# Two engines take up the first tile's copies and shares ahead of splitting the first expert's first chunk

## The chip, the cores and the metric
The kernel runs on one core of a Trainium2 chip. The metric is the device time of one execution in microseconds (us), as the median of several; the profile is of one further execution. The five engines run their own instruction streams and meet only at semaphores: TensorE (PE, with its weight loads shown as PEld), VectorE (DVE), ScalarE (ACT), GpSimd (POOL) and SyncE (SP, which here only issues transfers). Each engine takes its instructions in the order in which the program gives them, so an instruction that waits holds up all that stands behind it on its engine.

## The reference
1024 rows (32 batches of 32) of width 1024 go through three blocks. Each adds its result to the rows.

```python
def _L0_attn_ref(minibatch, eta):                 # the second block, "mixing"
    logits = jnp.einsum('bcl,bdl->bcd', minibatch, minibatch)
    logits_new = jnp.max(logits, axis=-1, keepdims=True) - logits
    probs = jax.nn.softmax(logits_new, axis=-1)
    read = jnp.einsum('bcd,bdl->bcl', probs, minibatch)
    return eta * read + minibatch

x = x + _L0_xattn_ref(_layernorm(x), ctx_4096, ctx_4096, Wq, Wk, Wv, Wo)
x = x + _L0_attn_ref(_layernorm(x), eta)
x = x + _L0_ffn_ref(_layernorm(x), gate_w, expert_w)   # 8 experts, the best 2 of each row
```

The first block is cross attention over a context of 257 rows a batch, the last a mixture of eight experts, each a 1024 x 1024 product.

## The kernel before
All products that matter are made from float32 split in two parts of less precision, a high one (a rounded copy, made by ACT) and a low one (what is left, a subtraction on DVE), and three passes: high by high, high by low, low by high. `attend` is the attention up to its output projection. `finish` does the rest for eight tiles of 128 rows (NT = 8), and this case lies in its first loop, the mixing stage. Every engine runs that loop over t and in each step serves up to three tiles at once, in an order written out by hand:

- PE (from `for t in range(1, NT)`): the output projection of tile t, `product(t, unit)`, in eight units of six matmuls of 512 columns (L1554). Between the units stand, for earlier tiles, `mix(t - 2)` ahead of unit 2 (L1588, L1594), `turn_y(t - 1)` ahead of unit 4 (eight transposes, L1566), `rank(t - 2)` ahead of unit 5 and `products_of_rows(t - 1)` ahead of unit 6 (64 small matmuls, L1578). `turn_y` writes the turned rows to PSUM, `products_of_rows` needs them in SBUF, as yT.
- ACT (L1277 on): `ot_high(t + 1)` splits the next tile's attention output (L1221), `first_high(0, t - 1)` makes the high part of one 128 x 1024 chunk of the first expert's weights (L1256), `copy_y(t - 1)` copies the turned rows to yT (L1228), `exp_gap`, `normalize_n`, then `shares(t - 1)` takes the exponentials of the products (L1244).
- DVE (L1455 on): the second half of x2 = x + projection (`add_x(t - 1, 1)`, L1338), its moments (L1344, L1348), `normalize_y` (L1353), the mixing sum and the routing of tile t - 2, `ot_low(t + 1)` (L1329), `first_low(0, t - 1)`, which is the low part of the expert's chunk (L1438), `add_x(t, 0)`, `rank_tile(t - 2)` and `turn_shares(t - 1)`, which takes the least product of each row (low, L1418), waits for ACT's exponentials, turns them (probT, L1424) and makes the scales up to L1432.
- SP: after the attention four small loads of the gate's weights into yT (L1035), one of eta (L1036), a clearing store, then the eight chunks of the first expert (L1025), and from there one row tile of x a step (`load_x(t + 1)`, L1022).
- POOL: the powers for the norms, the sum of x2 and y, and the scattering of routing entries.

`first_high(0, 0)` waits until chunk 0 of the expert has been loaded. The loads of the expert can't start before the attention is over, since they use its memory. At t = 1 there is no tile t - 2 yet, so `mix`, `rank` and their partners on the other engines fall away.

After the mixing stage the rows are gathered by expert and multiplied, tile by tile (L1624 for the first three tiles, L1708 for the others, with transposes at L1615).

Of the kernel before, what the change touches and what calls it, by code (L numbers as in the profile page):

```python
# [29 lines left out]
NT = B * SQ // P  # L30
# [858 lines left out]
def finish(nc, sh, x, eta, gate, expert_w, out, n_dram, slot_dram):  # L889
# [6 lines left out]
    with ExitStack() as ctx:  # L896
# [91 lines left out]
        def on(t, lag):  # L988

            return 0 <= t - lag < NT  # L990
# [226 lines left out]
        def _(act):  # L1217
            def ot_high(t):
                if t >= 2:
                    act.wait_ge(xo_done, 2 * t - 2)  # L1220
                act.activation(ot[0][:, t % 2, :, :], oT[:, t, :, :], ACT.Copy).then_inc(ot_h_ready, 1)  # L1221

            def copy_y(t):
                if t >= 1:
                    act.wait_ge(g_done, t)
                for h in range(2):
                    act.wait_ge(t_done, 2 * t + h + 1)
                    act.activation(yT[:, 4 * h:4 * h + 4, :, 0:SQ], t_ps[h][:, :].rearrange("p (k b q) -> p k b q", k=4, q=SQ),  # L1228
                                   ACT.Copy).then_inc(t_copied, 1)

            def exp_gap(t):
                act.wait_ge(gap_ready, t + 1)
                act.wait_ge(rstd3_ready, t + 1)
                act.activation(egap[:, :], gap[:, :], ACT.Exp, scale=rstd3[:, 0:1]).then_inc(egap_ready, 1)

            def normalize_n(t):
                if t >= 2:
                    act.wait_ge(x3_stored[t % 2], 32 * (t // 2))
                act.wait_ge(shift3_ready, t + 1)
                act.activation(n[:, t % 2, :], x3[:, t % 2, :], ACT.Identity, bias=shift3[:, 0:1], scale=rstd3[:, 0:1]).then_inc(n_ready, 1)  # L1240

            def shares(t):
                act.wait_ge(low_ready, t + 1)
                act.activation(prob[:, :], g_ps[:, 0:SQ], ACT.Exp, bias=low[:, 0:1], scale=-1.0,  # L1244
                               accum_out=psum_row[:, :]).then_inc(prob_ready, 1)

            def first_high(e, *chunks):
                for c in chunks:
                    if e == 0:
                        if c == 0:  # L1250
                            act.wait_ge(xo_done, 2)
                        act.wait_ge(ot_l_ready, c + 1)
                    else:
                        act.wait_ge(xo_done, 2 * NT)
                    act.wait_ge(chunk_loaded[c], 48 + 16 * e)
                    act.activation(w[0][:, e * SLOT + c * D:e * SLOT + (c + 1) * D], first_raw[e][:, c, :], ACT.Copy).then_inc(w_h_ready, 1)  # L1256

            def rows_high(i, par):
                if known(i) and i < 2:
                    act.wait_ge(xo_done, 2 * NT - 2 + 2 * i)  # L1260
                else:
                    act.wait_ge(y_done, 2 * i - 2)
                for h in range(2):
                    act.wait_ge(gT_done, 2 * i + h + 1)
                    act.activation(gT[0][:, par, h * 512:(h + 1) * 512], t_ps[h][:, :], ACT.Copy).then_inc(gT_h_ready, 1)  # L1265
# [11 lines left out]
            for t in range(NT + 2):  # L1277
                if 1 <= t and t + 1 < NT:
                    ot_high(t + 1)
                if 1 <= t < NT:  # L1280
                    first_high(0, t - 1)
                if t == NT - 1:
                    first_high(0, NT - 1)
                if t == NT:
                    rows_high(0, 0)
                if on(t, 1):
                    copy_y(t - 1)
                if on(t, 2):
                    exp_gap(t - 2)
                    normalize_n(t - 2)  # L1290
                if on(t, 1):
                    shares(t - 1)
                if t == NT:
                    first_high(1, 0, 1, 2, 3)
# [31 lines left out]
        def _(dve):  # L1326
# [4 lines left out]
            def add_x(t, h):  # L1331
                par = t % 2
                cols = slice(h * 512, (h + 1) * 512)
                dve.wait_ge(x_loaded[par], 16 * (t // 2) + 16)
                if t >= 2:
                    dve.wait_ge(u_ready, 2 * t - 2)
                dve.wait_ge(xo_done, 2 * t + h + 1)
                dve.tensor_tensor(x2[:, par, cols], o_ps[h][:, :], x_in[:, par, cols], ALU.add).then_inc(x2_ready, 1)  # L1338

            def moments(t):  # L1340
                par = t % 2
                for h in range(2):
                    dve.wait_ge(x2_ready, 2 * t + h + 1)
                    dve.bn_stats(stats2[:, h, :], x2[:, par, h * 512:(h + 1) * 512]).then_inc(stats2_ready, 1)  # L1344
                dve.wait_ge(stats2_ready, 2 * t + 2)
                if t >= 1:
                    dve.wait_ge(std_ready, t)
                dve.bn_aggr(mean_var2[:, :], stats2[:, :, :].rearrange("p a b -> p (a b)")).then_inc(var2_ready, 1)  # L1348
# [63 lines left out]
            def turn_shares(t):  # L1412
                par = t % 2
                if t == 0:
                    dve.wait_ge(consts, 16)
                    dve.wait_ge(small_loaded, 16 * (BT + 1))
                dve.wait_ge(g_done, t + 1)
                dve.tensor_reduce(low[:, :], g_ps[:, 0:SQ], AXX, ALU.min).then_inc(low_ready, 1)  # L1418
                dve.wait_ge(prob_ready, t + 1)
                if t >= 1:  # L1420
                    dve.wait_ge(mix_done, t)
                for b in range(BT):
                    q = slice(b * SQ, (b + 1) * SQ)
                    o = dve.transpose(probT[q, q], prob[q, :])  # L1424
                o.then_inc(probT_ready, 1)
                dve.tensor_tensor(gated[:, par, :], g_ps[:, SQ:GW], zero8[:, :], ALU.add).then_inc(gated_ready, 1)
                dve.wait_ge(std_ready, t + 1)
                dve.tensor_tensor(scaled_gated[:, par, :], g_ps[:, SQ:GW], std_plus_one[:, par, :].to_broadcast([P, E]),
                                  ALU.mult).then_inc(gated_ready, 1)
                dve.reciprocal(scale[:, par, :], psum_row[:, :]).then_inc(psr_ready, 1)  # L1430
                dve.wait_ge(psr_ready, t + 1)
                dve.tensor_tensor(scale[:, par, :], scale[:, par, :], eta_sb[:, :], ALU.mult).then_inc(scale_ready, 1)  # L1432

            def first_low(e, *chunks):
                for c in chunks:
                    high, rest = (part[:, e * SLOT + c * D:e * SLOT + (c + 1) * D] for part in w)
                    dve.wait_ge(w_h_ready, KC * e + c + 1)
                    dve.tensor_tensor(rest, first_raw[e][:, c, :], high.bitcast(F32), ALU.subtract).then_inc(w_l_ready, 1)  # L1438
# [10 lines left out]
            def rows_low(i, par):  # L1449
                for h in range(2):  # L1450
                    dve.wait_ge(gT_h_ready, 2 * i + h + 1)
                    dve.tensor_tensor(gT[1][:, par, h * 512:(h + 1) * 512], t_ps[h][:, :],  # L1452
                                      gT[0][:, par, h * 512:(h + 1) * 512].bitcast(F32), ALU.subtract).then_inc(gT_l_ready, 1)

            for t in range(NT + 2):  # L1455
                if on(t, 1):
                    add_x(t - 1, 1)
                    moments(t - 1)
                    if t == EARLY + 2:
                        pad_first_tiles()  # L1460
                    if t == NT:
                        rows_low(0, 0)
                    normalize_y(t - 1)
                if on(t, 2):
                    add_mixed(t - 2)
                    route_tile(t - 2)
                if 1 <= t and t + 1 < NT:
                    ot_low(t + 1)
                if 1 <= t < NT:
                    first_low(0, t - 1)  # L1470
                if t < NT:
                    add_x(t, 0)
                if on(t, 2) and t < NT:
                    rank_tile(t - 2)
                if t == NT - 1:
                    first_low(0, NT - 1)
                if on(t, 1):
                    turn_shares(t - 1)
                if t == NT:
                    first_low(1, 0)  # L1480
                if t >= NT:
                    rank_tile(t - 2)
                if t == NT:
                    first_low(1, 1)
# [270 lines left out]
```

## Time and profile before

| | |
|---|---|
| median of 3 runs | 1076.35 us (1076.14 to 1076.91) |
| the profiled execution | 1077.07 us, of which its span (first to last instruction) 1075.4 us |
| busy: PE / PEld | 1046.3 us (97%) / 957.9 us (89%) |
| busy: DVE / ACT / POOL | 630.2 (59%) / 477.4 (44%) / 242.3 us (23%) |
| mean granted TensorE clock | 0.992 of full speed |

A row of a timeline gives the start in us from the span's first instruction, the duration in us, the engine, the line, the operation, what it writes and reads, its count, and in brackets how long its engine sat idle before it and what ended that. The chain of waits is followed back from the last instruction: at each point, what released the work that stood there. Matmuls are pipelined, and their durations overlap; the distance from start to start says more than a duration.

### The profile page before, as it was taken

How to read it: one execution, taken by the hardware profiler on the slowest of the kernel's cores; microseconds unless marked ns; L12 is line 12 of the kernel's file. 1: busy time of each engine (PE TensorE's matmuls, PEld its weight loads, DVE VectorE, ACT ScalarE, POOL GpSimd, SP SyncE). 2: the span in 40 equal slices, each digit the busy share in tenths (PEclk: the TensorE clock that was granted, in tenths of full speed). 3: DMA queues.
4: the chain of work that ended last, by engine and by line, in shares of the span. 5: the costliest groups of instructions: out<-in, count | busy, mean ns of one | idle time of the engine just before them, and what ended most of it. 6: DMA issues, size and time to landing. Idle time of an engine off the chain costs nothing.

```text
span 1075.4 us, 25383 instructions
## 1 busy us (share of the span) xinstructions
PE 1046.3 (97%) x9043; PEld 957.9 (89%) x9044; DVE 630.2 (59%) x1623; ACT 477.4 (44%) x1129; POOL 242.3 (23%) x412
## 2 busy tenths in 40 slices
PE   9999999999999999999999999899997899999996
PEld 9999999999999999999999999677775788888885
DVE  6641366666666666666766668757778244354220
ACT  4321255455555545555555555523235154454331
POOL 2000212121212121121212121135444323322232
PEclk9999999999999999999999999999999899999998
DMA  9424686656565757575756757365537677588332
GB/s 345 140 79 154 182 246 190 173 184 181 176 192 171 199 171 202 156 209 157 207 155 200 226 152 199 85 238 99 91 127 235 198 227 256 132 259 254 87 77 38
DMA packets 78603, 189.46 MB, mean 176 GB/s; under 512 B 16512, under 2 KB 27136, under 8 KB 74400
## 3 DMA queue, kind: packets, MB, share of 16 engines
q1 hardware_dynamic: 64096, 154.15, 46.6%
q0 software_dynamic: 14400, 33.88, 13.0%
q8 instruction: 69, 1.13, 0.5%
q14 instruction: 38, 0.31, 0.1%
HBM read 148.66 MB, written 44.56 MB: 180 GB/s over the span
## 4 chain that ended last, share of the span: by engine, by line
PE 90%; DMA 3%; DVE 3%; issue 2%; POOL 1%; ACT 1%; SPq 0%; POOLq 0%; DVEq 0%; ACTq 0%
PE bank L1708 18%; PE bank L728 17%; PE bank L719 17%; PE bank L680 9%; PE bank L1554 6%; PE bank L767 6%; PE bank L711 5%; PE bank L786 4%; PE bank L856 3%; PE bank L1615 2%; PE bank L1624 1%; DMA xg<-n_scratch,idx 1%; DMA expert_raw<-in_expert_w 1%; PE bank L756 1%; PE bank L1588 1%
## 5 line engine op out<-in xcount | busy, mean ns | idle before, releaser
L487 ACT ACTIVATE prob<-bank,nmax 128x257 f32<-128x257 f32 x256 | 122.1, 477 | 235.7 <-DVE nmax L635 235.7
L635 DVE TENSOR_REDUCE nmax<-bank 128x1 f32<-128x257 f32 x256 | 108.9, 425 | 151.8 <-PE bank L856 151.8
L728 PE MATMUL bank<-wkv_h,cT_h 128*128 128x256 f32 x512 | 154.5, 302 | 0.0
L719 PE MATMUL bank<-cT_h,wkv_h 128*128 128x256 f32 x512 | 154.3, 301 | 0.0
L728 PE MATMUL bank<-wkv_h,cT_l 128*128 128x256 f32 x512 | 144.6, 282 | 0.0
L719 PE MATMUL bank<-cT_h,wkv_l 128*128 128x256 f32 x512 | 144.3, 282 | 0.0
L728 PE MATMUL bank<-wkv_l,cT_h 128*128 128x256 f32 x512 | 144.1, 282 | 0.0
L719 PE MATMUL bank<-cT_l,wkv_h 128*128 128x256 f32 x512 | 144.0, 281 | 0.0
L382 POOL DMA_DIRECT2D qcat<-q_scratch x128 | 70.5, 557 | 271.5 <-PE bank L856 268.4
L1708 PE MATMUL bank<-w_h,rows_h 128*128 x272 | 108.7, 400 | 0.0
L1708 PE MATMUL bank<-w_l,rows_h 128*128 x272 | 107.3, 394 | 0.0
L1708 PE MATMUL bank<-w_h,rows_l 128*128 x272 | 107.3, 394 | 0.0
L767 PE MATMUL bank<-ident,prob 128*128 128x128 f32 x512 | 99.6, 276 | 3.6 <-DVE pT L273 1.9
L1452 DVE TENSOR_TENSOR rows_l<-bank,rows_h 128x512 fp32r<-128x512 f32 x42 | 27.0, 684 | 127.5 <-ACT rows_h L1265 127.4
L728 PEld LDWEIGHTS bank<-wkv_h,cT_h 128*128 128x128 f32 x512 | 97.4, 190 | 0.0
L627 DVE TENSOR_SCALAR prob<-prob,rsums 128x257 f32<-128x257 f32 x256 | 92.0, 359 | 9.1
L719 PEld LDWEIGHTS bank<-cT_l,wkv_h 128*128 128x128 f32 x512 | 97.2, 190 | 0.0
L728 PEld LDWEIGHTS bank<-wkv_l,cT_h 128*128 128x128 f32 x512 | 97.1, 190 | 0.0
L719 PEld LDWEIGHTS bank<-cT_h,wkv_h 128*128 128x128 f32 x512 | 96.9, 189 | 0.0
L719 PEld LDWEIGHTS bank<-cT_h,wkv_l 128*128 128x128 f32 x512 | 96.8, 189 | 0.0
L728 PEld LDWEIGHTS bank<-wkv_h,cT_l 128*128 128x128 f32 x512 | 96.7, 189 | 0.0
L569 DVE TENSOR_TENSOR cT_l<-bank,cT_h 128x512 fp32r<-128x512 f32 x128 | 87.1, 682 | 10.1 <-ACT cT_h L442 10.1
(213 smaller groups left out, 2377.2 us busy)
## 6 DMA issues: line engine op xcount, KB each, us to landing
kcat<-k_scratch SPq DMA_DIRECT2D x128, 258.0 KB, 4.4
cx<-in_context SPq DMA_DIRECT2D x32, 1024.0 KB, 6.8
raw<-in_expert_w SPq DMA_DIRECT2D x48, 512.0 KB, 7.3
qcat<-q_scratch POOLq DMA_DIRECT2D x128, 128.0 KB, 3.1
k_scratch<-kT_h SPq DMA_DIRECT2D x32, 258.0 KB, 2.4
k_scratch<-kT_l SPq DMA_DIRECT2D x32, 258.0 KB, 2.6
x_in<-in_x SPq DMA_DIRECT2D x16, 512.0 KB, 7.6
expert_raw<-in_expert_w SPq DMA_DIRECT2D x16, 512.0 KB, 8.1
```

The lines of the kernel that those rows point to most:

```text
L382: pool.dma_start(qcat[c * DH:(c + 1) * DH, par, :, :].rearrange("d (g j) n -> d g (j n)", g=4).bitcast(F32), q_dram[c // 2, b].rearrange(" ...
L487: act.activation(prob[1 - par][:, s, 0:SK], s_ps[s % 2][:, 0:SK], ACT.Exp, bias=nmax[:, 1 - par, s:s + 1], accum_out=sums[:, 1 - par, s:s ...
L569: dve.tensor_tensor(cT[1][:, b % 2, 2 * m:2 * m + 2, :].rearrange("p a n -> p (a n)"), cT_ps[m % 2][:, :], high, ALU.subtract).then_inc(cT ...
L627: dve.tensor_scalar(prob[a % 2][:, i, 0:SK], prob[a % 2][:, i, 0:SK], rsums[:, i:i + 1], None, ALU.mult).then_inc(prob_ready, 1)
L635: dve.reduce_max(nmax[:, 1 - par, s:s + 1], s_ps[s % 2][:, 0:SK], AXX, negate=True).then_inc(max_done, 1)
L680: o = pe.matmul(q_ps(UNITS * g + u)[:, m % 2 * GT:(m % 2 + 1) * GT], wq_s[w][:, k, m * P:(m + 1) * P], xT[g % 2][t][:, k, :], start=(m % 2 ...
L711: o = pe.transpose(cT_ps[m % 2][:, n * P:(n + 1) * P], cx[:, b % 2, a, k * P:(k + 1) * P], ident[:, :])
L719: o = pe.matmul(k_ps[:, j * 256:(j + 1) * 256], wkv[w][:, k, j * P:(j + 1) * P], cT[t][:, b % 2, k, :], start=(j == 0 and k == 0 and n == ...
L728: o = pe.matmul(v_ps[:, a * KV:(a + 1) * KV], cT[t][:, b % 2, k, a * P:(a + 1) * P], wkv[w][:, k, KV:2 * KV], start=(a == 0 and k == 0 and ...
L767: o = pe.transpose(turn_ps[:, c * P:(c + 1) * P], prob[a % 2][:, i, c * P:(c + 1) * P], ident[:, :])
L1554: o = pe.matmul(o_ps[h][:, :], ot[a][:, t % 2, k, :], wo_s[b][k][:, h * 512:(h + 1) * 512], start=(k == 0 and m == 0), stop=(k == KC - 1 a ...
L1708: o = pe.matmul(y_ps[par][h][:, :], gT[a][:, par, k * P:(k + 1) * P], w[b][:, bass.ds(slot_at + (k * D + h * 512), 512)], start=(k == 0 an ...
```

## The change
On ACT and on DVE, in step t = 1 alone, the split of the first expert's chunk 0 moves behind other work. ACT now does `copy_y(0)` and then `first_high(0, 0)`, ahead of `shares(0)`. DVE now does `first_low(0, 0)` at the end of the step, behind `add_x(1, 0)` and `turn_shares(0)`. From t = 2 on the order is the old one. No instruction is added or removed.

```diff
@@ ScalarE
-                if 1 <= t < NT:
+                if 2 <= t < NT:
                     first_high(0, t - 1)
                 if t == NT - 1:
                     first_high(0, NT - 1)
@@
                 if on(t, 1):
                     copy_y(t - 1)
+                if t == 1:
+                    first_high(0, 0)
                 if on(t, 2):
                     exp_gap(t - 2)
                     normalize_n(t - 2)
@@ VectorE
                 if 1 <= t and t + 1 < NT:
                     ot_low(t + 1)
-                if 1 <= t < NT:
+                if 2 <= t < NT:
                     first_low(0, t - 1)
                 if t < NT:
                     add_x(t, 0)
@@
                 if on(t, 1):
                     turn_shares(t - 1)
+                if t == 1:
+                    first_low(0, 0)
                 if t == NT:
                     first_low(1, 0)
```

## Rows read from the trace of the kernel before

**Rows 1.** The page, chain that ended last: shares of the span by engine.
```profile
PE 90%; DMA 3%; DVE 3%; issue 2%; POOL 1%; ACT 1%; SPq 0%; POOLq 0%; DVEq 0%; ACTq 0%
```

**Rows 2.** Windows: busy us of each engine (instructions), clock, DMA share, GB/s.
```profile
703.95:706.28 2.33, 0.07 (x1) 0.00 (x0) 0.99 (x1) 2.03 (x3) 0.00 (x0) 1.00 1.02 417
706.28:711.46 5.18, 5.18 (x77) 4.18 (x78) 2.30 (x11) 0.38 (x2) 0.00 (x0) 0.67 1.03 418
711.46:726.80 15.34, 15.34 (x132) 11.89 (x131) 12.14 (x38) 4.79 (x8) 6.87 (x10) 1.00 0.36 134
```

**Rows 3.** Timeline of PE, steps t = 1 and t = 2 of mixing.
```profile
700.19 1.03 PE L1566 MATMUL bank<-ident,y 128*128 128x128 f32 x8
...
703.62 0.40 PE L1554 MATMUL bank<-wo_h,rows_l 128*128 128x512 f32 x1
706.28 0.80 PE L1578 MATMUL bank<-yT 128*32 128x40 f32 x64 [2.27 <-ACT yT L1228]
...
711.46 0.40 PE L1554 MATMUL bank<-wo_h,rows_h 128*128 128x512 f32 x1
...
714.25 1.88 PE L1588 MATMUL bank<-y,probT 128*128 128x512 f32 x4
...
718.97 1.03 PE L1566 MATMUL bank<-ident,y 128*128 128x128 f32 x8
...
722.85 0.40 PE L1554 MATMUL bank<-wo_h,rows_l 128*128 128x512 f32 x1
723.18 0.80 PE L1578 MATMUL bank<-yT 128*32 128x40 f32 x64
...
726.79 0.39 PE L1554 MATMUL bank<-wo_h,rows_h 128*128 128x512 f32 x1
```

**Rows 4.** Timeline of ACT, the same two steps.
```profile
704.20 1.06 ACT L1256 ACTIVATE w_h<-expert_raw 128x1024 fp32r<-128x1024 f32 x1 [8.22 <-DMA expert_raw<-in_expert_w]
...
719.67 1.09 ACT L1228 ACTIVATE yT<-bank 128x512 f32<-128x512 f32 x2 [6.00 <-PE bank L1566]
...
724.25 0.29 ACT L1244 ACTIVATE prob<-bank,low 128x32 f32<-128x32 f32 x1 [2.19 <-DVE low L1418]
```

**Rows 5.** Timeline of DVE, the same two steps.
```profile
705.29 1.22 DVE L1438 TENSOR_TENSOR w_l<-expert_raw,w_h 128x1024 fp32r<-128x1024 f32 x1 [5.84 <-ACT w_h L1256]
...
711.73 0.69 DVE L1338 TENSOR_TENSOR x<-bank,x_in 128x512 f32<-128x512 f32 x1 [2.47 <-PE bank L1554]
...
714.85 0.81 DVE L1353 TENSOR_SCALAR y<-x,mean_var,rstd 128x1024 f32<-128x1024 f32 x1 [1.00 <-POOL rstd L1101]
...
724.03 0.19 DVE L1418 TENSOR_REDUCE low<-bank 128x1 f32<-128x32 f32 x1 [0.22 <-PE bank L1578]
...
725.89 0.16 DVE L1432 TENSOR_TENSOR scale<-scale,eta_sb 128x1 f32<-128x1 f32 x1
```

**Rows 6.** Timeline of SP: issues of the transfers around the change.
```profile
697.58 0.58 SPq L1036 DMA_DIRECT2D eta_sb<-in_eta  x1
...
703.15 9.62 SPq L1022 DMA_DIRECT2D x_in<-in_x  x2
```

**Rows 7.** Transfers issued from 685 to 730 us: size, median us to landing.
```profile
x_in<-in_x SPq DMA_DIRECT2D x3, 512.0 KB, 10.0
...
eta_sb<-in_eta SPq DMA_DIRECT2D x1, 0.5 KB, 3.0
```

**Rows 8.** The chain of waits after the mixing stage: start, us, what.
```profile
799.07 9.97 DMA xg<-n_scratch,idx
```

**Rows 9.** Timeline of PE after the mixing stage: two of its idle times.
```profile
824.45 0.39 PE L1598 MATMUL bank<-both,earlier 128*128 128x8 f32 x2 [2.08 <-DVE both L1395]
...
844.68 1.97 PE L1615 MATMUL bank<-ident,xg 128*128 128x128 f32 x8 [2.92 <-DMA xg<-n_scratch,idx]
```

**Rows 10.** Windows of L1624 alone: PE and PEld busy us, clock, DMA share, GB/s.
```profile
832.20:841.80 9.60, 9.56 (x40) 7.45 (x40) 1.00 0.02 3
...
844.70:856.00 11.30, 9.66 (x32) 7.47 (x32) 0.74 0.99 304
```

## The prediction
> **What bounds the kernel now.** I read the page's chain first, then the stretch around the change in windows, then PE, ACT, DVE and SP one by one in order of time. PE holds 90% of the chain that ended last [rows 1], so time is won where PE stands still or runs slowly, and nearly nowhere else. In the mixing stage a full step is 15.34 us, in which PE is busy for all 15.34 us at clock 1.00 [rows 2]. Step t = 1 is different. PE reaches its products of rows and stands idle for 2.27 us, until ACT has copied the turned rows [rows 3]. After this, from 706.28 to 711.46, the granted clock is 0.67 in the mean [rows 2]: part of the stretch is at the lower of the two levels (1.2 GHz), the rest at 2.4 GHz. Why is the copy late? ACT sat idle for 8.22 us, up to 704.20, until chunk 0 of the expert had landed [rows 4]. The copy stands behind that split in ACT's order, although the transposes that it reads started at 700.19 [rows 3]. DVE likewise was idle for 5.84 us, from 699.45 to 705.29, for the low part of the same chunk [rows 5]. So at this place a transfer that PE doesn't need before the first expert product, after all eight steps, decides when PE goes on.
>
> **Part 1: the copy goes ahead of the split (ACT).** In the next step the copy starts 719.67 - 718.97 = 0.70 us after the first transpose and lasts 1.09 us for its two halves [rows 3, 4]. In step 1 it would run from 700.19 + 0.70 = 700.89 to 701.98. ACT is free by then, since its idle time began at 704.20 - 8.22 = 695.98 [rows 4]. PE wants yT one step of matmuls after 703.62. In the undisturbed step the distance from the last matmul to the products of rows is 723.18 - 722.85 = 0.33 us, in step 1 it was 706.28 - 703.62 = 2.66 us [rows 3]. The difference, **2.33 us**, is the stall, and it goes whole: PE starts its products at 703.95, and yT has been there for 1.97 us.
>
> What is late next at 703.95? These products also wait for the gate's and eta's small loads. Eta's is the last of them to be issued, at 697.58 [rows 6], and took 3.0 us [rows 7], so it is there at 700.6 (701.2 if the 3.0 us count from the end of the issue). That leaves at least 2.8 us, and I cost it at nothing. Were it later than 703.95, every us would be one of stall.
>
> **Part 2: the slow clock.** From the first product of rows to the first matmul of the next tile it is 726.79 - 723.18 = 3.61 us at full clock, and 711.46 - 706.28 = 5.18 us in step 1, for the same instructions [rows 3]. The difference is **1.57 us**. (From the mean clock the loss would be (1 - 0.67) x 5.18 = 1.71 us [rows 2]; the distances are the better measure, and 0.14 us goes into the range.) Up to the stall the engine was busy and the clock 1.00; the clock was low only after it. I take it that without the stall the clock stays at 1.00. No row shows step 1 without a stall, so its bounds are 0 and 1.57 us; I take 1.57, since the window of the next step, with the same work and no idle time, is at 1.00 for all of 15.34 us [rows 2]. It isn't settled by idle time alone: an idle time of 2.08 us before 824.45 [rows 9] is the nearest one and has no slow stretch behind it (the 40 matmuls that follow it are at clock 1.00 [rows 10]), while the one of 2.92 us before 844.68 [rows 9] is followed by a mean clock of 0.74 over 11.3 us [rows 10].
>
> The Trainium skill (TensorE: Matmul & The Clock Gate, Part 1) says that the monitor behind the clock runs free of the kernel, and that one kernel can show different numbers of slow matmuls in different runs. By that the term of this part could be anything from 0 to 1.57 us in a given run, and the sum from 2.33 to 3.90 us. The three times before lie within 0.77 us, less than half of 1.57 us, which speaks for a slow stretch in each of them.
>
> **Part 3: what is moved back.** ACT: chunk 0's high part can start when it did, at 704.20, and ends at 705.26 [rows 4]. `shares(0)` stands behind it. It would be wanted 0.22 us after low starts (724.25 - 724.03), and low starts 724.03 - 723.18 = 0.85 us after the products of rows [rows 3 to 5]: low at 704.80, shares at 705.02, but ACT is free at 705.26 only. That is 0.24 us late. From shares to the last scale it is 725.89 + 0.16 - 724.25 = 1.80 us [rows 4, 5], so to 707.06. PE wants the turned shares for `mix(0)` at 714.25 - 3.90 = 710.35 [rows 3]: 3.3 us to spare, which hides the 0.24 us.
>
> DVE: `first_low(0, 0)` now runs behind that, from 707.06 to about 708.2 (1.22 us, less a little overlap [rows 5]). Behind it stands `add_x(1, 1)`, which was released by PE at 711.73 and would now be at 707.83; so it starts 0.37 us late, at 708.2. From its start to the end of y it takes 714.85 + 0.81 - 711.73 = 3.93 us [rows 5], to 712.13; POOL's power lies within this. PE wants y for its transposes at 718.97 - 3.90 = 715.07 [rows 3]. That is 2.9 us to spare, so this too costs nothing. `add_x(1, 0)`, which had stood behind chunk 0, comes earlier. In the next step DVE waits for PE by only 0.22 us at low [rows 5], so the 0.37 us may show there as 0.15 us, but PE takes its shares only a mix later and doesn't see it.
>
> SP: no transfer is moved in its order. The load of x's tile 2 is issued at 703.15 as before, and lands after about 10.0 us, at 713.15 [rows 6, 7]. Its reader comes in the three us ahead of the low of the next step, which is to start at 724.03 - 3.90 = 720.13 [rows 5], so from 717.1 on: about 4 us of cover. The following tile's load is released by `add_x(1, 1)`, so some 3.5 us earlier, behind the expert's last chunks. Chunk 1 is wanted by ACT about 3.9 us sooner than before. Should it land later, only the next copy stands behind it, wanted at 719.67 - 3.90 = 715.77 [rows 4]. POOL has nothing moved.
>
> **Sum.** 2.33 + 1.57 = **3.90 us**. Control from one pair of distances: 711.46 - 703.62 = 7.84 us in step 1 against 726.79 - 722.85 = 3.94 us in the next [rows 3]. All that follows is released by what stands before it: even the gather of 9.97 us in the chain at 799.07 [rows 8] starts when earlier rows are routed, so it moves with the rest, and each further chunk of the expert is wanted a step of 15.3 us after the one before [rows 2]. I see nothing later that is tied to the clock on the wall, and carry the whole 3.90 us to the end. The profiled execution took 1077.07 us (span 1075.4, so 1.67 us around it) and would take 1073.17, with a span of 1071.5. It lies 0.72 us above the median of the runs, which becomes 1076.35 - 3.90 = **1072.45 us** (-0.36%).
>
> **The rivals.**
> 1. The slow clock stays (it comes from something else than the stall, such as the transfers at 418 GB/s beside it [rows 2]). Then 2.33 us are won: 1074.0. Against: the transfers were as dense during the stall (417 GB/s, clock still 1.00).
> 2. The later clock changes with the shift. After the mixing stage PE has several idle times, and only one has a slow stretch behind it. That one costs (1 - 0.74) x 11.3 = 2.9 us [rows 10]. Part of this may go: 1071.0 if half of it does. Or the 2.08 us [rows 9] gets a slow stretch of the size of part 2: 1074.0. The free-running monitor of the page named above would do either by chance. By the trace I can't tell which; the narrow spread of the runs speaks against both.
> 3. Slower than before: the clock falls behind the idle time of 2.08 us and stays low through the second tile. Its 40 matmuls from 832.20 to 841.80 take 9.6 us, so 0.24 us each [rows 10], and at half clock twice that, 9.6 us more: 1082.05. It decides from 3.90 / 0.24 = 16 such slow matmuls on. Against: after 2.92 us of idle the loss was 2.9 us, which is 12 of these.
> 4. The change doesn't do what it says, since the products of rows wait for something else up to 706.28 (a small load under the expert's 4 MB): 1076.35, less whatever part of the 2.33 us is won. Against: PE's wait ended with ACT's copy [rows 3], and [rows 6, 7].
>
> **How the numbers follow.** My forecast has 0.77, rival 1 has 0.06, rival 2 has 0.10 (half on either side), rival 3 has 0.03, rival 4 has 0.04. The forecast alone would lie from 1071.7 to 1073.3: the 0.14 us of part 2, the spread of the runs, and that a transfer lands differently without a profile, which changes the length of the stall that is won. The range takes in rival 2's gain and rivals 1 and 2 at 1074.0: 1070.9 to 1074.2. A measurement of this kernel can tell about 0.2% (2.15 us) from no change, so from 1074.2 down it is faster. The forecast and nearly all of rivals 1 and 2 lie there, at 0.90; within 0.2% are rival 4 and the edges of the others, 0.07; slower 0.03.
>
> **What would show it.** In the profile after: ACT's copy at 700.9 with PE as its releaser, and chunk 0's split after it at 704.2; no idle time of PE at L1578, which starts at about 703.95; clock 1.00 from 700 to 716; the next tile's first L1554 at about 707.56; DVE's w_l at 707 to 708; a span of about 1071.5. I am wrong if L1578 still has idle time (rival 4), if L1578 starts at 703.95 and the next tile later than 708.5 (rival 1), or if the next tile starts at 707.6 and the span isn't 3.9 us shorter (rivals 2 and 3: then the clock in the stretch from 816 to 852 differs).

## The result, and the profile after

| | before | changed |
|---|---|---|
| median of 10 runs each | 1077.06 us (1074.93 to 1081.85) | 1072.95 us (1070.85 to 1075.48) |
| ratio | | 0.9955, 95% interval 0.994 to 0.997 |
| profiled execution, span | 1077.07 us, 1075.4 us | 1075.41 us, 1073.9 us |

By the ratio the change makes the kernel 0.45% faster (4.9 us, by the interval 3.2 to 6.5 us); the two medians lie 4.1 us apart. The forecast was 3.9 us, or 0.36%. The spread of the ten runs is much wider than that of the three times shown at first: 6.9 us before and 4.6 us changed.

The page of the changed kernel, parts 1 and 4 (busy time, and the chain that ended last, to set beside [rows 1]):

```profile
PE 1045.3 (97%) x9043; PEld 956.7 (89%) x9044; DVE 630.0 (59%) x1623; ACT 477.5 (44%) x1129; POOL 242.1 (23%) x412
...
PE 92%; DVE 3%; issue 2%; DMA 2%; POOL 1%; ACT 0%; POOLq 0%; SPq 0%; DVEq 0%; ACTq 0%
```

The share of PE rises by two points and that of DMA falls by one: the load of the expert's chunk has left the chain. Lines of the code have moved by up to four numbers (the projection L1554 is now L1558, the products of rows L1578 are L1582). The timelines of the changed kernel, first PE, which answers to [rows 3]:

```profile
706.95 0.40 PE L1558 MATMUL bank<-wo_h,rows_l 128*128 128x512 f32 x1
707.27 0.80 PE L1582 MATMUL bank<-yT 128*32 128x40 f32 x64
...
710.89 0.39 PE L1558 MATMUL bank<-wo_h,rows_h 128*128 128x512 f32 x1
...
718.41 1.03 PE L1570 MATMUL bank<-ident,y 128*128 128x128 f32 x8
```

ACT, which answers to [rows 4]:

```profile
704.15 1.09 ACT L1228 ACTIVATE yT<-bank 128x512 f32<-128x512 f32 x2 [4.86 <-PE bank L1570]
707.88 1.06 ACT L1256 ACTIVATE w_h<-expert_raw 128x1024 fp32r<-128x1024 f32 x1 [2.64 <-DMA expert_raw<-in_expert_w]
708.85 0.27 ACT L1244 ACTIVATE prob<-bank,low 128x32 f32<-128x32 f32 x1
```

DVE, which answers to [rows 5]:

```profile
703.79 0.69 DVE L1340 TENSOR_TENSOR x<-bank,x_in 128x512 f32<-128x512 f32 x1 [1.03 <-PE bank L1558]
...
709.24 0.85 DVE L1426 STREAM_TRANSPOSE probT<-prob 32x32 f32<-32x32 f32 x4 [0.82 <-ACT prob L1244]
...
710.54 1.22 DVE L1440 TENSOR_TENSOR w_l<-expert_raw,w_h 128x1024 fp32r<-128x1024 f32 x1
711.68 0.69 DVE L1340 TENSOR_TENSOR x<-bank,x_in 128x512 f32<-128x512 f32 x1
```

In this execution the mixing stage's first projection starts at 697.83 instead of 694.50, because the attention ran 3.33 us longer. Take 3.33 off every number and the forecast can be laid on it. PE goes from 706.95 to its products at 707.27 without a bracket: no idle time. ACT is released for the copy by PE's transposes and no longer by a DMA, and only then waits 2.64 us for chunk 0, with nothing urgent behind it. From the last matmul ahead of the products to the next tile it is 710.89 - 706.95 = 3.94 us, where it was 7.84 us.

The span is only 1.5 us shorter, though. Three pieces make it up, read from the first projection, from the next tile's first matmul, and from the end:

| profiled execution | chip | attention, to the first projection | the stretch of the change, to the next tile | rest | span |
|---|---|---|---|---|---|
| before | not recorded | 694.50 | 16.96 | 363.94 | 1075.4 |
| changed | not recorded | 697.83 | 13.06 | 363.01 | 1073.9 |
| changed, second | 12 | 696.24 | 13.08 | 365.48 | 1074.8 |
| ACT's part alone | 12 | 695.69 | 13.78 | 366.23 | 1075.7 |
| DVE's part alone | 12 | 696.47 | 16.10 | 367.63 | 1080.2 |
| before, stall filled | 12 | 695.95 | 15.87 | 365.88 | 1077.7 |
| before, once more | 1 | 694.87 | 16.30 | 363.43 | 1074.6 |
| changed, third | 1 | 695.29 | 13.08 | 362.33 | 1070.7 |
| before, chunk 0 issued first | 1 | 695.50 | 13.07 | 362.43 | 1071.0 |

The first column moves by 3.3 us and the third by 5.3 us. Most of the latter lies between the chips: on chip 12 the rest takes 365.5 to 367.6 us, on chip 1 it takes 362.3 to 363.4. The middle column repeats within 0.02 us for the same changed code, on either chip. So the change is judged from the middle column and from times taken on one chip, and not from two spans.

### The profile page after: what moved, and what is told of

Same layout as the page of the kernel before. It is cut to its first block, busy times and chain, and to the rows that moved or that the text cites. A ratio compares the mean times of both kernels' runs of the same rounds, so it can differ in the third digit from the quotient of the medians.

```text
span 1073.9 us, 25383 instructions
## 1 busy us (share of the span) xinstructions
PE 1045.3 (97%) x9043; PEld 956.7 (89%) x9044; DVE 630.0 (59%) x1623; ACT 477.5 (44%) x1129; POOL 242.1 (23%) x412
## 4 chain that ended last, share of the span: by engine, by line
PE 92%; DVE 3%; issue 2%; DMA 2%; POOL 1%; ACT 0%; POOLq 0%; SPq 0%; DVEq 0%; ACTq 0%
PE bank L1712 18%; PE bank L719 16%; PE bank L728 16%; PE bank L680 9%; PE bank L1558 8%; PE bank L767 6%; PE bank L711 5%; PE bank L786 4%; PE bank L856 3%; PE bank L1619 2%; PE bank L1628 1%; PE bank L756 1%; PE bank L1592 1%; PE bank L1570 1%; DMA kcat<-k_scratch 1%
## 5 line engine op out<-in xcount | busy, mean ns | idle before, releaser
L442 ACT ACTIVATE cT_h<-bank 128x512 fp32r<-128x512 f32 x128 | 76.6, 599 | 36.9 <-PE bank L711 36.9
```

Of the source, the lines that this page charges most:

```text
L442: act.activation(cT[0][:, b % 2, 2 * m:2 * m + 2, :].rearrange("p a n -> p (a n)"), cT_ps[m % 2][:, :], ACT.Copy).then_inc(cT_h_ready, 1)
```

## The experiments

The runs were made in three groups, each on one chip with its own runs of before; a ratio is always to before on the same chip. The medians of before were 1080.48 us on chip 12 (each engine's part, the filled stall, the changed kernel again), 1074.89 us on chip 10 (chunk 0 loaded last, the first filled gather) and 1076.63 us on chip 1 (the others), so times of different groups can't be set side by side.

### Each engine's part alone

ACT's order changed, DVE's as it was:

```diff
 # ScalarE only
-                if 1 <= t < NT:
+                if 2 <= t < NT:
                     first_high(0, t - 1)
...
                     copy_y(t - 1)
+                if t == 1:
+                    first_high(0, 0)
```

> ACT's part of the change alone: the copy of the turned rows ahead of the split of chunk 0, DVE in its old order. My theory (the stall and the slow clock both come from ACT's order): the whole gain, 3.9 us against before; PE has no idle time at the products of rows, and from the last matmul ahead of them to the first of the next tile it takes 3.94 us (7.84 in before). DVE waits for chunk 0 up to about 705.3, so low is about 2 us later than with both parts, and the last scale is at about 709.4, still 0.9 us ahead of the mixing product at 710.35. Rival (DVE's order matters too, since the sum behind its split comes late and the shares miss the mixing product): some 1 to 2 us less gain, with idle time of PE at the mixing product.

Ratio 0.9962 (0.9948 to 0.9976). The timeline of PE of this kernel, and then that of DVE:

```profile
709.47 0.47 PE L1556 MATMUL bank<-wo_h,rows_h 128*128 128x512 f32 x1 [0.53 <-DVE x L1340]
```

```profile
707.50 1.23 DVE L1440 TENSOR_TENSOR w_l<-expert_raw,w_h 128x1024 fp32r<-128x1024 f32 x1 [6.87 <-ACT w_h L1256]
708.64 0.69 DVE L1340 TENSOR_TENSOR x<-bank,x_in 128x512 f32<-128x512 f32 x1
```

Nearly all of the gain is ACT's, but not all. The stretch takes 13.78 us instead of 13.07: PE stands idle for 0.53 us, and not at the mixing product, as the rival had it, but at the next tile's first matmul. That one writes the bank that `add_x(1, 0)` must have read, and on DVE this sum stands behind the low part of chunk 0. So DVE's part is worth about 0.7 us by the traces. The times (0.9962 against 0.9955 for both parts on the same chip) point the same way, but their intervals overlap, so they don't show it.

DVE's order changed, ACT's as it was:

```diff
 # VectorE only
-                if 1 <= t < NT:
+                if 2 <= t < NT:
                     first_low(0, t - 1)
...
                     turn_shares(t - 1)
+                if t == 1:
+                    first_low(0, 0)
```

> DVE's part of the change alone, ACT in its old order. My theory: nothing, within 0.3 us of before, since the copy still stands behind chunk 0 on ACT: the distance from the last matmul ahead of the products of rows to the next tile's first stays at 7.8 us. Rival (DVE's idle time of 5.84 us was worth something by itself): up to 1 us faster.

Ratio 0.9992 (0.9978 to 1.0007): nothing, as expected, since the copy still waits on ACT. What I had not expected stands in its windows, below: a stall of 2.96 us with no low clock behind it.

### Does the stall bring the low clock?

The kernel before, with ten matmuls in the place of the idle time:

```diff
             def products_of_rows(t):
+                if t == 0:
+                    for _ in range(10):
+                        pe.matmul(r_ps[0][:, :], ot[0][:, 1, 0, :], wo_s[0][0][:, 0:512], start=True, stop=True)
                 pe.wait_ge(t_copied, 2 * t + 2)
```

> The kernel before, with ten matmuls of 512 columns on PE (10 x 0.2325 = 2.33 us, into an unused bank) in the place of the idle time ahead of the first products of rows; their result isn't used. ACT still copies late. My theory (the idle time brings the low clock): PE reaches the products at the same time as before, 706.3, with no or little idle time, the clock stays at 1.00 from 706 to 712, and the next tile starts 1.57 us earlier than in before: 1.57 us faster in all. Rival (the low clock comes from the transfers beside it, or from the engine's load as a whole): the clock still falls, and the time is that of before.

Ratio 0.9978 (0.9964 to 0.9993), so 2.4 us less, 0.8 to 3.9 by the interval. Its timeline of PE:

```profile
705.30 2.50 PE L1573 MATMUL bank<-wo_h,rows_h 128*128 128x512 f32 x10
708.19 0.51 PE L1581 MATMUL bank<-yT 128*32 128x40 f32 x33 [0.39 <-ACT yT L1228]
```

The filling did what it should: 0.39 us of idle time is left, and the clock is 1.00 behind it (708.19 to 711.82). A gain appears although no product comes sooner, which speaks for the clock. But the kernel before, run once more and profiled, and DVE's part alone had no low clock behind their stalls either. The kernel before once more:

> The kernel before against itself, for the size of a null result and for a second profile of the stall. The kernel with DVE's part alone had a stall of 2.96 us with no low clock behind it. My first theory (the stall brings the low clock) wants a mean clock of 0.6 to 0.8 from 706 to 712 here too. The rival, by now the likelier (the clock falls after such a stall in some executions only): a stall of 2.3 to 3 us, and the clock may be 1.00 behind it. Ratio 1.000 within 0.0015 in both.

Ratio 1.0003 (0.9983 to 1.0022), so the comparison has no lean. Its timeline of PE, with the longer stall, and of ACT:

```profile
707.53 0.80 PE L1578 MATMUL bank<-yT 128*32 128x40 f32 x64 [3.15 <-ACT yT L1228]
```

```profile
705.45 1.06 ACT L1256 ACTIVATE w_h<-expert_raw 128x1024 fp32r<-128x1024 f32 x1 [9.12 <-DMA expert_raw<-in_expert_w]
```

The windows from the first product of rows to the next tile (busy us of the engines, then clock, DMA share, GB/s), of before once more, of DVE's part alone, and of the kernel before with chunk 0 loaded last, whose stall is 11.04 us; [rows 2] has the one of before, at 0.67:

```profile
707.53:711.17 3.64, 3.64 (x76) 3.04 (x77) 2.31 (x11) 0.38 (x2) 0.00 (x0) 1.00 1.03 419
```

```profile
708.94:712.57 3.63, 3.63 (x76) 3.05 (x77) 2.13 (x10) 0.38 (x2) 0.00 (x0) 1.00 1.02 419
```

```profile
716.54:722.19 5.65, 5.65 (x77) 4.68 (x77) 2.31 (x11) 0.38 (x2) 0.00 (x0) 0.59 0.01 3
```

Stalls of 3.15 and 2.96 us were followed by full clock, one of 2.27 us by a low one. So behind 2 to 3 us of idle time the clock fell in some executions and not in others; behind 11 us, in one profile, it fell. The transfers are neither needed for the low clock nor enough for it: at 419 GB/s the clock was 1.00, at 3 GB/s it was 0.59.

How often the low clock came in the other runs can be read in part, since the mean granted clock of every run is on record. A stretch like that of [rows 2] takes 0.0016 off it, which is (1 - 0.67) x 5.18 us out of 1075. On chip 12 the filled stall had a mean of 0.994 or more in 10 of 12 runs, before in 4 of 30, and the averages are 0.9944 and 0.9917. So slow stretches were frequent in before there, and with the stall filled they cost less by more than one stretch of this size; where in the execution they lay is not recorded. The two profiles with full clock behind the stall, at 0.994 and 0.995, belong to the better runs of their kernels: 4 of 12 reached as much in each.

### Is chunk 0's landing the whole cause, and how much cover has it?

The kernel before with chunk 0 loaded last:

```diff
-            for c in range(KC):
+            for c in (1, 2, 3, 4, 5, 6, 7, 0):
                 load_first(0, c)
```

> The kernel before, with chunk 0 as the last of the expert's eight loads. My theory (the copy waits for chunk 0 and nothing else): the stall at the products of rows grows by what chunk 0 lands later, 8.7 us, to about 11 us, and the slow stretch behind it lasts at least as long: 9 to 11 us slower than before. Rival (another small load or the transposes end the stall): the stall stays near 2.3 us.

Ratio 1.0092 (1.007 to 1.0114), 9.9 us slower. The timeline of PE:

```profile
716.54 1.29 PE L1578 MATMUL bank<-yT 128*32 128x40 f32 x64 [11.04 <-ACT yT L1228]
```

The stall follows the landing one for one. The split of chunk 0 started 18.47 us after the first projection (714.46 - 695.99) instead of 9.70 us in the first profile of before, and both this and the stall are 8.77 us longer. The same edit in the changed kernel:

> The changed kernel with chunk 0 as the last of the expert's eight loads. It then lands some 7 x 1.25 = 8.7 us later, at about 712.8 instead of 704.1 (4 MB at 420 GB/s take 10 us). The shares stand behind its split on ACT. My theory (3.3 us to spare at the mixing product, then one for one): ACT's shares end near 714.2, the turned shares are ready near 715.2, and PE, which wants them at 710.35, stands idle for about 4.8 us and then has a low clock for 1.6 us or more: 6 us slower than the changed kernel, so about 2.5 us slower than before. Rival (there is more cover than I think): no more than 1 us slower than the changed kernel.

Ratio 1.0035 (1.0021 to 1.0048), 3.8 us slower than before where about 2.5 were expected. The timeline of ACT, then of PE:

```profile
713.34 1.06 ACT L1256 ACTIVATE w_h<-expert_raw 128x1024 fp32r<-128x1024 f32 x1 [11.37 <-DMA expert_raw<-in_expert_w]
```

```profile
715.69 3.65 PE L1592 MATMUL bank<-y,probT 128*128 128x512 f32 x4 [5.12 <-DVE probT L1426]
```

The products of rows now run on time (704.00). The wait has moved to the mixing product, 5.12 us where 4.8 were expected: the shares stand behind the split. The cover is real but finite. With the split behind the shares too:

```diff
                     copy_y(t - 1)
-                if t == 1:
-                    first_high(0, 0)
...
                     shares(t - 1)
+                if t == 1:
+                    first_high(0, 0)
```

> As the one with chunk 0 loaded last, and on ACT the split of chunk 0 stands behind the shares too, so that only the next step's work stands behind the load. My theory: ACT is blocked up to 712.8, but what stands behind it on ACT is wanted at 715.8 only (the next copy). DVE's low part of chunk 0, though, stands ahead of the sum of tile 1 and the norm that PE wants at 715.07: the sum starts at about 715.1 instead of 708.2, y is ready at 719, and PE is idle for about 4 us at the transposes of the next step, plus a low clock: 4 to 6 us slower than the changed kernel. Rival (only ACT's order counts): as fast as the changed kernel.

Ratio 1.0039 (1.0027 to 1.0051), no better. The changed kernel itself wasn't run on this chip. With its mean gain of 4.0 us on the others (below), both kernels are some 8 us slower than it, more than the 6 and the 4 to 6 us expected, and the rest wasn't traced to a cause. The timeline of DVE, then of PE:

```profile
714.65 1.23 DVE L1440 TENSOR_TENSOR w_l<-expert_raw,w_h 128x1024 fp32r<-128x1024 f32 x1 [7.70 <-ACT w_h L1256]
```

```profile
719.78 1.97 PE L1570 MATMUL bank<-ident,y 128*128 128x128 f32 x8 [4.50 <-DVE y L1355]
```

The mixing product is on time (710.38), and the next thing on DVE is late: the sum and the norm behind the chunk's low part. The place and the size (4.50 us, about 4 expected) are those of the forecast. Three orders, three places where the same late chunk stops PE.

Last, the cause itself removed in the kernel before, with both old orders:

```diff
             sp.wait_ge(sh.pv_done, B)
+            sp.wait_ge(xo_done, 2)
+            load_first(0, 0)
             for b in range(BT):
                 sp.dma_start(yT[:, :, b, SQ:GW], ...)
...
-            sp.wait_ge(xo_done, 2)
-            for c in range(KC):
+            for c in range(1, KC):
                 load_first(0, c)
```

> The kernel before, with both old orders, and on SP the load of chunk 0 moved ahead of the gate's and eta's small loads and the clearing store, so that it is issued about 4 us sooner, at 694.6 instead of 698.7. My theory (chunk 0's landing was the whole cause): it lands before 701, its split is over by about 702, the copy by 703.2, PE has no idle time at the products of rows: the same gain as the change, 3.9 us. Rival (the small loads, now 0.6 us later, become the last to land): PE or DVE waits for them up to about 704.5, and the gain is 0.5 to 1 us smaller.

Ratio 0.9972 (0.9955 to 0.999), beside 0.9978 for the changed kernel on that chip. The timeline of ACT:

```profile
699.28 1.07 ACT L1257 ACTIVATE w_h<-expert_raw 128x1024 fp32r<-128x1024 f32 x1 [2.31 <-DMA expert_raw<-in_expert_w]
701.82 1.09 ACT L1229 ACTIVATE yT<-bank 128x512 f32<-128x512 f32 x2 [1.47 <-PE bank L1567]
```

The split is over before the transposes are, and the stretch takes 13.07 us, the same as with the change. Moving one load does what moving the work does.

### The changed kernel again, and the wait after the mixing stage

> The changed kernel once more, for the size of the gain and for how far its profile moves from one execution to another. My theory: 3.9 us less than before in the median; in the stretch of the change no idle time and 3.94 us from the last matmul ahead of the products of rows to the next tile's first; what differs between executions lies elsewhere (the attention, and the low clock after the mixing stage). Rival (the change itself makes the later part worse by tying it to other transfers): a slow stretch at 820 to 830 again, and the distance from the end of the mixing stage to the end about 2 us longer than in before.

> The changed kernel a third time, as the mate of the filled gather on the same chip. My theory: ratio to before 0.9955 again (0.994 to 0.997), no idle time and clock 1.00 in the stretch of the change; PE's wait for the gather of the third tile anywhere from 3 to 7 us, set by how long the last routing entries take to land. Rival: a ratio above 0.997 on this chip.

Ratios 0.9955 (0.9938 to 0.9972) and 0.9978 (0.9962 to 0.9994). The second lies outside the 0.994 to 0.997 expected and is what the rival said; its wait for the gather was 2.53 us, also outside the 3 to 7 us. The intervals overlap, so it is open whether the chips differ in the gain. The mean of all three ratios is 0.9963, that is 4.0 us of 1077. The slow stretch came back after the idle time at the last ranking, as the rival of the first of these two runs had it. The 2 us by which it expected the rest to grow didn't show: on chip 12 the rest was 365.48 us, the shortest of the four there. The timeline of PE of the changed kernel, first profile:

```profile
822.50 0.39 PE L1602 MATMUL bank<-both,earlier 128*128 128x8 f32 x2 [2.06 <-DVE both L1397]
...
829.02 1.04 PE L1619 MATMUL bank<-ident,xg 128*128 128x128 f32 x8
```

The same of the kernel before, once more:

```profile
822.65 0.39 PE L1598 MATMUL bank<-both,earlier 128*128 128x8 f32 x2 [2.08 <-DVE both L1395]
827.61 1.04 PE L1615 MATMUL bank<-ident,xg 128*128 128x128 f32 x8
```

It is the same work in 829.02 - 822.50 = 6.52 us or 827.61 - 822.65 = 4.96 us: 1.56 us lost. A slow stretch came here in all three profiles of the changed kernel, in both with the filled gather (in one of them 8.04 us, so 3.08 us lost) and in that with chunk 0 issued first, and in none of the five in which PE had an idle time in the stretch of the change (3.15 us down to 0.39 us). Of those with chunk 0 last, one had it, with 3.08 us lost, and two had not. Six of six against none of five would be rare by chance, but no run tests what links the two places. The windows of 819.8 to 829.4 of the changed kernel and of before once more show it as clock:

```profile
819.80:829.40 9.60, 7.54 (x31) 5.88 (x30) 7.86 (x30) 6.11 (x7) 4.84 (x6) 0.82 1.07 235
```

```profile
819.80:829.40 9.60, 6.76 (x36) 5.22 (x34) 8.37 (x32) 6.93 (x10) 4.96 (x6) 1.00 1.06 241
```

In these profiles it cost nothing that reaches the end, since PE soon after waits for a gather anyway (3.23 us in the changed kernel), and that is released by POOL. In the chain of waits POOL stands in one piece between the last scattering of entries and the load of the indices. Of the changed kernel, and then of DVE's part alone:

```profile
827.60 9.10 issue
```

```profile
829.65 12.40 issue
```

The chain of the changed kernel with chunk 0 last names it, with 7.47 us:

```profile
833.02 7.47 DMA slot_scratch<-entries,slot
```

It is the landing of the last routing entries. In the profiles in which this piece shows it lasted from 7.11 to 12.40 us. It goes with the chip more than with the kernel: 10.31 to 12.40 us on chip 12, 8.44 to 9.37 us on chip 1, 7.11 to 7.47 us on chip 10, in the order of the medians of before. So it makes much of the 5.3 us by which the rest of the kernel moves.

The idle time in front of that gather, filled in the changed kernel:

```diff
                     if h == 1:
+                        pe.wait_ge(gated_ready, 2 * NT)
+                        for _ in range(12):
+                            pe.matmul(g_ps[:, :], gT[0][:, 1, 0:P], w[0][:, SLOT:SLOT + 512], start=True, stop=True)
                         turn_rows(2, 0)
```

> The changed kernel with twelve matmuls of 512 columns on PE (2.8 us, result unused) ahead of the transposes of the third tile, where PE stood idle for 2.92 us in before and 3.23 us in the changed kernel's profile, waiting for a gather. My theory (the low clock follows idle time): no low clock in the first product of the second tile's second half and of the third tile, so up to 2.9 us less than the changed kernel, at least 1 us. Rival (the clock falls anyway, or the filling work delays what matters): the same time as the changed kernel or up to 1 us more.

> The changed kernel with twelve matmuls ahead of the transposes of the third tile once more, now beside the changed kernel on the same chip. By its first look (no low clock from 840 to 856, but one from 816 to 832, and no idle time at those transposes) my theory is that the filling keeps the clock where it stands but that its 2.8 us are lost in those executions in which the gather is there already; in the median 0 to 1.5 us less than the changed kernel. Rival (the filling work costs more than the clock gives): 1 to 2 us more.

Ratios 0.9974 (0.996 to 0.9989) on a chip where the changed kernel wasn't run, and 0.9958 (0.9939 to 0.9977) beside 0.9978 for the changed kernel. The timeline of PE of the second:

```profile
843.91 1.09 PE L1619 MATMUL bank<-ident,xg 128*128 128x128 f32 x8 [0.59 <-DMA xg<-n_scratch,idx]
852.32 1.03 PE L1619 MATMUL bank<-ident,xg 128*128 128x128 f32 x8
```

From these transposes to the next ones it takes 852.32 - 843.91 = 8.41 us, against 10.01 us in the changed kernel's third profile (841.16 to 851.17): the clock stays up. The median is 1.3 us lower than that of the changed kernel on this chip, but the intervals overlap. Whether this beats the changed kernel isn't settled.

## Why the prediction was right, step by step

- **What bounds: right.** PE waited for the copy, the copy for the split, the split for the load. Loading chunk 0 sooner gives the same 13.07 us in the stretch, loading it last costs 9.9 us.
- **Part 1, the stall of 2.33 us: right in kind, small in size.** It is gone in each of the profiles with ACT's part. The one profile of before had the shortest stall, 2.27 us of idle time; others had 2.96 and 3.15. The reason is in the landing: chunk 0 was there 9.70 us after the first projection in that profile (704.20 - 694.50) and 10.58 us in the next (705.45 - 694.87), and the stall grew by the same 0.88 us. The term should have been about 2.9 us with some 0.5 us on either side.
- **Part 2, the slow clock of 1.57 us: too large for two of three profiles, open for the median.** I took it in full by the window of the next step, and let the three times of before, within 0.77 us, speak for a slow stretch in each. Ten runs of before spread over 6.9 us, so this agreement was luck and carried no weight. In the two further profiles with a stall of this length the clock didn't fall, so in these the changed order wins 16.30 - 13.07 = 3.23 and 16.10 - 13.07 = 3.03 us, where the first won 3.89. The mean clocks of the runs (above) say that slow stretches were common in before all the same. In these two profiles one term was too small where the other was too large; that the sum came so near to the median is in part luck. The free-running monitor of the Trainium skill (TensorE: Matmul & The Clock Gate, Part 1), which I had left at the edge, fits these rows: the same code, the same place, clock 0.67 once and 1.00 once. The monitor itself shows in no row, and chance alone would not give the split of six against none at the last ranking.
- **Part 3, what is moved back: right on ACT, a gap on DVE.** With 3.33 us taken off, the split started at 704.55 (forecast 704.20), the last sum at 708.35 (708.2) and the transposes at 715.08 (715.07). Shares cost 0.37 us of waiting on DVE more than in a full step (0.82 against 0.45 us), forecast 0.24 us; no one on PE saw it. The forecast gave DVE's part no price, and passed over `add_x(1, 0)` with "comes earlier". Without it PE loses 0.7 us at the next tile. I had looked for who waits for the shares, and not for who waits for the bank.
- **The carry to the end: not contradicted, and invisible in one pair of profiles.** On the one chip where both were profiled again, the rest of the kernel took 363.43 us in before and 362.33 us in the changed kernel; in the first pair it was 363.94 and 363.01 us. So nothing of the gain was lost behind the stretch in these pairs. The mean of the three ratios, 4.0 us, agrees with the 3.90.
- **Rivals.** The first (the transfers cause the low clock) fell. The second happened in part: a new slow stretch of 1.56 us after the last ranking, but in the shade of the gather. The third asked for 9.6 us lost at that place and didn't happen; the fourth didn't either. "A span of about 1071.5" was the wrong test: it missed by 2.4 us while each point of the stretch held.

## What to carry to other kernels

A wait at the head of an engine's queue is paid by everything behind it, so put the work that feeds the busiest engine ahead of the work whose input is still on its way, or issue that one transfer sooner. Ask of each moved instruction which buffer it frees as well as which value it makes. And judge a change of some us from the stretch where it acts, over several profiles, with before and changed on the same chip: here the stretch repeated within 0.02 us while the span moved by 4.1 us.

## What the runs showed of the hardware

- After idle times of 2 to 3 us TensorE's granted clock fell in some executions and stayed in others: 2.27 us and a mean of 0.67 behind it, 2.96 and 3.15 us and 1.00. The idle time at the last ranking was 2.06 to 2.09 us in all fourteen profiles. In seven the same work behind it took 4.95 to 4.97 us, in five 6.52 or 6.53 us, in two 8.04 us.
- A pair of indirect scatters of routing entries took from 7.11 to 12.40 us from the last issue to the next step of POOL. The loads of the second expert were over by then in the changed kernel's profile (issued from 808.34 to 812.09, at most 11.2 us to landing, the scatters from 824.35). What ran beside them was a 512 KB store of normalized rows. It took 11.5 to 12.4 us to land on chip 1 and 12.9 to 16.1 us on chip 12, so it was slow where the scatters were. Which of them holds up the other was not tested.
- In the kernel with chunk 0 issued first, the low part of a chunk on DVE fell together with POOL's sum of x2 and y. Its timelines, DVE and then POOL:

```profile
700.38 2.29 DVE L1439 TENSOR_TENSOR w_l<-expert_raw,w_h 128x1024 fp32r<-128x1024 f32 x1
```

```profile
699.38 4.43 POOL L1117 TENSOR_TENSOR x<-x,y 128x512 f32<-128x512 f32 x2
```

  The first takes 1.22 us elsewhere [rows 5], so it nearly doubled. POOL's took 2.53 or 2.54 us in the later steps of this kernel, and 3.44 us at this place in before. Which resource they share was not tested, and it cost nothing here, since DVE then waited 2.63 us for PE.
